# Both halves of some transposed probability tiles copied by ScalarE in a two-layer transformer kernel

## The reference

```
xn = layernorm(x);  x = x + latent_attention(xn) + experts_top2(xn)     # layer 1
xn = layernorm(x);  x = x + flow_attention(xn)   + experts_top4(xn)     # layer 2
```

```
scores = einsum('bhsd,bhtd->bhst', q, k) * scale          # 1024 x 1024 per head
attn   = softmax(scores, axis=-1)
o      = einsum('bhst,bhtd->bhsd', attn, v_c)
```

## Time and profile before

| | |
|---|---|
| timed runs | 2602.13, 2607.09, 2613.08 us; median 2607.09 us |
| profiled execution | 2604.15 us, its span 2602.4 us |
| mean granted TensorE clock | 0.958 of full speed |
| PE busy | 2318.3 us, 89% of the span |
| PEld busy | 1679.3 us, 65% |
| DVE busy | 2080.8 us, 80% |
| ACT busy | 1600.3 us, 61% |
| POOL busy | 717.4 us, 28% |

### The profile page before, as it was taken

How to read it: one execution, slowest core, us unless ns; L and a number is a source line. 1 busy time by engine, 2 the same in 40 slices (tenths; PEclk the granted TensorE clock), 3 DMA queues, 4 the chain that set the end, 5 groups by cost and what they waited for, 6 DMA issues and landing times.

```text
span 2602.4 us, 65321 instructions
## 1 busy us (share of the span) xinstructions
PE 2318.3 (89%) x25647; PEld 1679.3 (65%) x25647; DVE 2080.8 (80%) x3611; ACT 1600.3 (61%) x2890; POOL 717.4 (28%) x605
## 2 busy tenths in 40 slices
PE   6889988899888998889989899898998889988898
PEld 4667566675666766667656676566765666656675
DVE  6968878788787888788887878879778697796976
ACT  3756557665576655765566755667456584575845
POOL 2220432205322052221522215212252022520234
PEclk8999999999899998999999999899998999999999
DMA  7110221103111021111211112111121112211022
GB/s 253 42 37 7 94 63 42 41 2 113 44 42 41 17 104 38 46 37 43 82 34 47 37 46 87 32 48 29 62 75 33 43 30 73 68 34 47 20 74 65
DMA packets 99128, 141.38 MB, mean 54 GB/s; under 512 B 11524, under 2 KB 60621, under 8 KB 98317
## 3 DMA queue, kind: packets, MB, share of 16 engines
q1 hardware_dynamic: 90636, 120.41, 14.8%
q0 software_dynamic: 8192, 16.79, 2.2%
HBM read 101.84 MB, written 31.13 MB: 51 GB/s over the span
## 4 chain that ended last, share of the span: by engine, by line
PE 52%; DVE 26%; issue 14%; ACT 7%; DMA 0%; SPq 0%; DVEq 0%; POOL 0%; ACTq 0%; POOLq 0%
PE ps L1515 10%; DVE neg_max L1175 10%; PE ps L1522 6%; PE ps L1597 5%; DVE probsT L1185 5%; PE ps L1687 4%; PE ps L1724 4%; ACT probs L797 3%; PE ps L1709 3%; PE ps L1619 3%; PE ps L1472 2%; DVE ffn L1315 2%; PE ps L1536 2%; PE ps L1488 2%; DVE key_low L953 2%
## 5 line engine op out<-in xcount | busy, mean ns | idle before, releaser
L797 ACT ACTIVATE probs<-ps,neg_max 128x1024 f32<-128x1024 f32 x512 | 571.1, 1116 | 187.0 <-DVE neg_max L1175 178.8
L1175 DVE TENSOR_REDUCE neg_max<-ps 128x1 f32<-128x1024 f32 x512 | 620.9, 1214 | 38.1 <-PE ps L1687 33.0
L1515 PE MATMUL ps<-shared,w_split 128*128 128x512 f32 x1536 | 467.7, 441 | 18.7 <-ACT ffn L848 11.7
L1709 PEld LDWEIGHTS ps<-ident,probs 64*128 64x128 f32 x8192 | 338.1, 145 | 120.3 <-issue 73.3
L685 POOL TENSOR_TENSOR probs<-ffn,shared 128x512 f32<-128x512 f32 x208 | 287.9, 1384 | 419.2 <-DVE ffn L1315 163.5
L1515 PEld LDWEIGHTS ps<-shared,w_split 128*128 128x128 f32 x1536 | 287.1, 192 | 166.4 <-issue 63.0
L1724 PE MATMUL ps<-probsT,latent 128*32 128x128 f32 x8192 | 331.3, 281 | 50.3 <-DVE o_latent L1168 49.5
L1687 PE MATMUL ps<-shared,query_a 64*128 64x512 f32 x1024 | 271.3, 526 | 117.6 <-ACT probs L797 95.2
L1709 PE MATMUL ps<-ident,probs 64*128 64x64 f32 x8192 | 359.0, 230 | 18.9 <-ACT probs L797 11.3
L1185 DVE COPY probsT<-ps 128x512 f32<-128x512 f32 x512 | 348.4, 681 | 19.5 <-PE ps L1709 17.7
L848 ACT ACTIVATE ffn<-ps,room_of_gate 128x512 f32<-128x512 f32 x256 | 175.1, 684 | 266.1 <-PE ps L1515 266.1
(11 more groups left out here) (229 smaller groups left out, 3437.8 us busy)
## 6 DMA issues: line engine op xcount, KB each, us to landing
w_split<-w_parts SPq DMA_DIRECT2D x132, 256.0 KB, 2.6
shared<-gate_rows SPq DMA_DIRECT2D x64, 512.0 KB, 4.3
y_rows<-probs SPq DMA_DIRECT2D x40, 256.0 KB, 2.2
x_in<-in_x SPq DMA_DIRECT2D x9, 512.0 KB, 4.1
out<-x_mid SPq DMA_DIRECT2D x8, 512.0 KB, 3.2
ffn<-in_gate_up SPq DMA_DIRECT2D x1, 2048.0 KB, 9.0
probsT<-in_gate_up SPq DMA_DIRECT2D x1, 2048.0 KB, 14.1
w_down<-in_down SPq DMA_DIRECT2D x2, 1024.0 KB
```

The lines of the kernel that those rows point to most:

```text
L797: nc.scalar.activation(probs[:, t % 3, :], banks(2 * (t % 2)), ACT.Exp, bias=neg_max[:, t % 4:t % 4 + 1], accum_out=row_sum[:, g % 2, t % ...
L1175: nc.vector.tensor_reduce(neg_max[:, t % 4:t % 4 + 1], banks(2 * (t % 2)), X, ALU.max, negate=True).then_inc(max_ready.sem, 1)
L1515: mm = nc.tensor.matmul(ps[:, bank, :], w_split[:, f % CHUNK_SLOTS, h, k * P:(k + 1) * P], tokens[:, half], start=(part == 0), stop=(part ...
L1709: mm = nc.tensor.transpose(ps[:, turn_bank(t, c), k * HQ:(k + 1) * HQ], probs[rows, t % 3, k * P:(k + 1) * P], ident[rows, rows])
```

## The change

In the first run of each sequence, for every second tile (odd i), and in the second run for every eighth (i % 8 = 7), ACT copies both halves: first the high half, then the low half. DVE's copy is left out for these tiles. So 16 tiles of 32 in the first run and 4 of 32 in the second change hands, 160 of the 512 in the program.

The semaphore high_copied now counts DVE's copies alone; the waits for it are recomputed by `on_dve(n)`, the number of DVE's copies among the first n tiles. For a tile of ACT low_copied stands for both halves, because ACT does the high half first. The work itself, its shapes and all other orders stay.

```diff
+def both_on_act(t):
+
+    run, i = divmod(t, NT * QUAD)
+    return i % 2 == 1 if run == 0 else i % 8 == 7
+
+
+def on_dve(n):
+
+    return sum(not both_on_act(t) for t in range(n))
...
-        high_copied = signal("high_copied", TILES)
+        high_copied = signal("high_copied", on_dve(TILES))
...
                             act.wait_ge(u_ready.sem, u_ready.at(b, t // QUAD - 1))
+                        if both_on_act(t):
+                            act.wait_ge(pT_high.sem, pT_high.at(b, t + 1))
+                            nc.scalar.copy(half_of(t, 1), half_turned(t, 1))
                         act.wait_ge(pT_low.sem, pT_low.at(b, t + 1))
                         nc.scalar.copy(half_of(t, 0), half_turned(t, 0)).then_inc(low_copied.sem, 1)
...
                     t = tile_of(w - T_LAG)
-                    if t is not None:
+                    if t is not None and not both_on_act(t):
                         if t >= 2 * QUAD:
...
-                pe.wait_ge(high_copied.sem, high_copied.at(b, NT * QUAD))
+                pe.wait_ge(high_copied.sem, high_copied.at(b, on_dve(NT * QUAD)))
...
-                        pe.wait_ge(high_copied.sem, high_copied.at(b, t - 1))
+                        pe.wait_ge(high_copied.sem, high_copied.at(b, on_dve(t - 1)))
...
-                        pe.wait_ge(high_copied.sem, high_copied.at(b, (g + 1) * QUAD))
+                        pe.wait_ge(high_copied.sem, high_copied.at(b, on_dve((g + 1) * QUAD)))
```

## The result

The changed kernel takes 2568.72 us (median of 4 runs, 2567.1 to 2571.41) against 2604.61 for the kernel before in the same comparison: a ratio of 0.9869, 95% interval 0.984 to 0.9898. The profiled execution has a span of 2567.0, 35.4 less than before. The forecast was 2560, so the direction and most of the size came, and 9 us of the forecast did not come.

The account below looks back on a forecast made before the run. DVE (VectorE) was taken as the bound. First-run terms 0.6 + 2.36 + 2.24 - 0.2 = 5.0 us a sequence, 40 for eight, plus 3 from the second run, off 2604.15 give 2561; forecast 2560, 8-in-10 range 2534 to 2586.

Parts of the forecast that it names:

- Entry: First run up to tile 10's scores: a wait for ACT's exp shrinks, 0.6 us gained a sequence, bounds 0 and 2.4.
- Tiles 10 to 18: First run: DVE stays the bound, so all four copies taken from it count, 2.36 us a sequence, low bound 1.2.
- Tiles 18 to 30: Late first run: four tiles gain 0.69 us; 2.24 over 13 steps to tile 31, bounds 0 and 3.35.
- PE comes to them at about 1.1 in one case and loses about 0.3 in the other: PE's transposes wait for an ACT tile's low half; costed at nothing, at most 0.3 us in four tiles.
- the forecast's 7.53: Late first run: time for four tiles after the change, in us, down from 8.22.
- ACT's chain behind the scale copy: Extra copy delays scale copy, DVE's product, next maximum and its exp; ACT waits 0.15 us once in four tiles.
- Handover: End of first run: the last tile's two copies run in sequence on ACT, PE's next stage waits; 0.2 us lost.
- Second run: Tiles 15 and 23 gain 0.3 us each, tile 7 loses about 0.2; 0.4 a sequence, 3 us in all.
- The rival that PE's floor is reached: Four tiles take 7.19 us and the entry gains too; 58 us off, 2546, or 2536; chance 0.24.
- The rival of ACT's order: PE's low-half waits add 0.3 us to a cycle, half of tiles 10 to 18's gain goes; 2581; chance 0.15.
- That the copies would cost more: Slower rival, in ACT's queue: instructions stop overlapping, four tiles take 9.18 us, total 2638; chance 0.07.
- 2569: Total in us if each ACT copy costs the skill page's 0.52 us; four tiles take 7.83; not adopted.

Follow-up runs that it names:

- the scale copy comes second: Against the kernel with low half first and second-run odd tiles from 13 on: ACT's scale copy moved between the two halves; 2564.24 us, ratio 0.9844.
- low half first: Against the changed kernel: ACT copies and signals the low half first, the high half after it under its own semaphore; 2566.88 us, ratio 0.9867.
- even tiles: Against the changed kernel: in the first run ACT takes even tiles instead of odd; 2572.32 us, and 2565.72 us with low half first as well.
- second run alone: Against the changed kernel: first run put back as before the change, only the second run's every eighth tile moved; 2604.1 us, ratio 0.9998.

## Why the prediction was nearly right

Per sequence, forecast against the profiled executions (medians; the pitch of 4.45 is a mean):

- **Entry: 0.6 forecast, 0.66 measured** from 2 to 10. As forecast, the wait ahead of tile 6's scores shrank, from 1.22 to 0.62. From maximum 2 to these scores there are 8.20 before and 7.60 after, and from there to maximum 10 12.02 and 11.97 (medians), so the copies taken from DVE behind the wait gave next to nothing. That the sum came so close is in part luck, since the second part alone moves by 0.9 with the granted clock (last section).
- **Tiles 10 to 18: 2.36 forecast, 2.15 measured.** DVE stayed the bound in all but the last step. There it waits for the scale copy (10 to 18 is 0.24 shorter where the scale copy comes second), which the prediction had considered only for the late stretch.
- **Tiles 18 to 30: 2.07 forecast (12 of the 13 steps), 1.56 measured.** This is the term that was mis-sized, and the step is "PE comes to them at about 1.1 in one case and loses about 0.3 in the other ... I cost that at nothing". The wait measured 0.42, more than the 0.34 that PE was thought to have to spare, and PE's delay then reached ACT, whose next copy waits for the transposes (1.22 after the exp, not 1.10). With 0.05 from the product, 1.35 after the first copy (737.15 to 738.50) and not 1.30, the forecast's 7.53 became 7.70. With the low half first the 0.12 is gone: 7.61, 0.08 over the forecast by the product alone; with even tiles that order takes 0.27 out. The mechanism that the term was built on, ACT's chain behind the scale copy, was right and is what low half first shows bare.
- **Handover: 0.2 lost forecast, 0.34 measured.** From ACT's first copy to PE's next stage there are 1.17 (752.36 to 753.53) and were 0.95, the 0.2 as worked out. The other 0.13 came ahead of them: the last exp starts at 749.76, 1.40 after its maximum at 748.36 and not 1.31, since two copies of tile 29 now stand in front of it, and the low half of tile 30, for which the last transposes wait, stands behind it, as it did before.
- **Second run: 0.4 gained forecast, 0.46 measured** (0.29 + 0.35 - 0.18). Tile 23's step is as worked out: product 1.25 after the first copy (1.30 forecast), transposes 1.16 (1.14).

These sum to 4.5 of the 5.4 forecast, and 8 x 4.45 = 35.6 is about the 35.4 us by which the span shrank. The second run's share can't be seen in a total: alone it can't be told from no change.

The rival that PE's floor is reached did not come (7.70, and 7.52 at best in the runs, against 7.19). The rival of ACT's order had the right mechanism, PE's wait for the low half, at less than half its size (0.12 of its 0.3 in four tiles by the rows, 0.08 by the run without the wait), and not in tiles 10 to 18. That the copies would cost more fell: the trace has neighbours 0.47 to 0.49 apart, even in the kernel with all copies on ACT. The Trainium skill's page "ScalarE: Activation LUTs", section "What ACT_TABLE_LOAD costs", gives an estimate of 0.52 us for such a copy, and the trace disagrees. That the total worked out from it, 2569, is what the kernel takes is luck: the missing time lies elsewhere, as said above.

## What to carry to other kernels

When work goes from a full engine to one with slack, write the new cycle with every engine's waits in one chain: a wait is free only while it is shorter than the slack left at the new pace. Here the slack was 0.34; the wait was taken for 0.3 and was 0.42. Signal first what the next engine needs first; the order of two copies on one engine was worth 0.27 us of 7.79 in the even tiles. And before an instruction is moved ahead of another, ask what it waits for: the extra copy that seemed in the way of the scale copy was filling a wait.

## What the runs showed of the hardware that was not expected

Durations of ACT's instructions grow when they follow each other without a gap, while their distance does not: the copies of low halves have a mean of 588 ns in the changed kernel and 623 in the one with all copies on ACT, where some last 0.68 to 0.72, and the copies that follow each other still start 0.47 to 0.49 apart. A busy time summed from durations overstates what they cost.

At the entry of the third sequence's first run PE's granted clock rose sooner in the changed kernel than before. The third to fifth window of 4 us from 692 on before, and from 684 on after, where the first maxima start at 692.47 and 684.10 (columns as in the earlier trace rows):

```profile
700.00:704.00 4.00, 1.85 (x38) 1.38 (x34) 3.97 (x6) 2.50 (x4) 0.00 (x0) 0.93 0.39 113
704.00:708.00 4.00, 3.56 (x38) 2.67 (x40) 3.93 (x7) 2.69 (x7) 0.00 (x0) 0.50 0.01 2
708.00:712.00 4.00, 4.00 (x72) 3.01 (x68) 3.61 (x8) 3.25 (x6) 0.00 (x0) 0.71 0.02 4
```

```profile
692.00:696.00 4.00, 2.45 (x40) 1.77 (x38) 3.93 (x7) 3.46 (x7) 0.00 (x0) 0.93 0.33 99
696.00:700.00 4.00, 4.00 (x60) 2.75 (x59) 3.53 (x6) 3.42 (x7) 0.00 (x0) 0.61 0.02 4
700.00:704.00 4.00, 4.00 (x89) 2.95 (x88) 3.76 (x9) 3.91 (x8) 0.00 (x0) 1.00 0.01 2
```

Before, PE is at the lower level (1.2 GHz) through the fourth window and reaches the upper (2.4 GHz) within the fifth; after, it changes within the fourth. In the window in which the clock fell PE had been busy 1.85 of 4 us before, and 2.45 after.

This is not the change's doing alone, as the clock differs between sequences of one kernel. Two windows of the kernel before, from tile 6's scores to maximum 10, in the third sequence and the fifth:

```profile
704.44:717.26 12.82, 12.82 (x186) 10.02 (x188) 10.85 (x20) 8.24 (x16) 0.00 (x0) 0.77 0.01 3
1341.99:1353.92 11.93, 11.83 (x186) 9.18 (x188) 10.77 (x21) 8.07 (x16) 0.00 (x0) 0.86 0.01 3
```

The same work takes 12.82 at a mean granted clock of 0.77 and 11.93 at 0.86 (in two more sequences 11.92 and 11.93, in the first 12.54). In the changed kernel six sequences have 0.86 and take 11.94 to 12.14, so at the same clock this part did not gain. In second run alone, whose first run is that of the kernel before, five sequences have 0.76 and take 12.92 to 12.95. In the third sequence the entry therefore shrank by 1.32, about 0.7 of it by the clock; the medians, 0.66, hold hardly any of it. Over eight sequences such a difference of 0.9 to 1.0 is 7 to 8 us, about the size of the 9 us that the forecast missed.
